# Last sums in two PSUM places, join preparation inside the edge pass, first gathers ahead of the row table

## The reference

```
x = x + gnn(layernorm(x), src, dst)      # 12 heads of 64
x = x + ffn(layernorm(x))

gnn: ft = h W per head;  e = leaky_relu(a1[src] + a2[dst], 0.2)
     w = exp(e - segment_max(e, dst)[dst]);  alpha = w / segment_sum(w, dst)[dst]
     out = relu(segment_sum(alpha * ft[src], dst) + h W_res)
ffn: rows 6..: gelu(x W1 + b1) W2 + b2;  rows 0..5: two gated experts each
```

## Time and profile before

| | us |
|---|---|
| median of 3 runs | 3018.57 |
| lowest, highest | 3011.17, 3021.54 |
| the profiled execution | 3011.33 |
| its span, first to last instruction | 3009.5 |

### The profile page before, as it was taken

The page is one execution under the profiler, slowest core; times in us unless marked ns, Lnnn a source line. Parts: engine busy times, 40 slices in busy tenths (PEclk is TensorE's granted clock), DMA queues, the critical chain, the costliest instruction groups (busy, mean ns, idle before and its releaser), DMA issues. The chain is left out here.

```text
span 3009.5 us, 65141 instructions
## 1 busy us (share of the span) xinstructions
PE 2853.7 (95%) x20124; PEld 2542.5 (84%) x20124; DVE 2488.2 (83%) x5828; ACT 1842.5 (61%) x3384; POOL 2120.1 (70%) x2027
## 2 busy tenths in 40 slices
PE   1999999999999994599999999999999999999998
PEld 1888888888888882488888998898998889898986
DVE  4799999999999966488888888888888888888884
ACT  0666666656566550466666766667666666666762
POOL 6766666666666600578888888888888888888882
PEclk9999999999999997699999999999999999999998
DMA  7999999888887825489888888888888888888873
GB/s 175 171 222 226 211 216 218 217 220 208 215 218 219 218 85 188 148 305 324 312 315 304 306 310 294 304 297 298 302 296 296 294 289 301 291 292 296 290 254 127
DMA packets 246617, 757.83 MB, mean 252 GB/s; under 512 B 78899, under 2 KB 81203, under 8 KB 246291
## 3 DMA queue, kind: packets, MB, share of 16 engines
q1 hardware_dynamic: 176644, 545.08, 51.2%
q0 software_dynamic: 69312, 209.33, 30.3%
q10 hardware_dynamic: 432, 0.62, 0.1%
HBM read 623.04 MB, written 232.17 MB: 284 GB/s over the span
## 5 line engine op out<-in xcount | busy, mean ns | idle before, releaser
L648 ACT ACTIVATE arena<-ps 128x768 f32<-128x768 f32 x392 | 317.9, 811 | 534.7 <-PE ps L708 533.5
L861 PE MATMUL ps<-wr_bd,arena 128*128 128x128 f32 x4704 | 598.4, 277 | 36.0 <-DVE arena L1180 34.6
L861 PEld LDWEIGHTS ps<-wr_bd,arena 128*128 128x128 f32 x4704 | 562.8, 193 | 45.7 <-issue 43.2
L840 PE MATMUL ps<-arena,w_sb 128*96 128x256 f32 x2352 | 571.6, 379 | 0.0
L571 POOL DMA_INDIRECT arena<-agg_scratch,nrow x392 | 439.5, 1121 | 77.7 <-issue 71.9
L1175 DVE SCALAR_TENSOR_TENSOR ps<-ps,r_n,arena 128x768 f32<-128x768 f32 x392 | 400.8, 1022 | 68.5 <-DMA arena<-agg_scratch,nrow 50.5
L840 PEld LDWEIGHTS ps<-arena,w_sb 128*96 128x96 f32 x2352 | 362.3, 163 | 82.8
L551 POOL TENSOR_SCALAR arena<-csr_neg,mv,r_n 128x768 f32<-128x768 f32 x392 | 387.5, 989 | 50.6 <-POOL r_n L579 39.9
L1180 DVE SCALAR_TENSOR_TENSOR arena<-ps,arena 128x768 f32<-128x768 f32 x392 | 375.3, 957 | 13.4
L563 POOL TENSOR_SCALAR arena<-arena,nm_n,r_n 128x768 f32<-128x768 f32 x392 | 383.8, 979 | 1.0 <-issue 0.4
L610 ACT ACTIVATE arena<-ps 128x512 f32<-128x512 f32 x588 | 312.1, 594 | 108.5 <-PE ps L725 70.4
(11 more groups left out here) (197 smaller groups left out, 5502.3 us busy)
## 6 DMA issues: line engine op xcount, KB each, us to landing
arena<-in_x SPq DMA_DIRECT2D x196, 768.0 KB
arena<-in_x_cols SPq DMA_DIRECT2D x392, 384.0 KB
out<-arena SPq DMA_DIRECT2D x195, 768.0 KB, 5.2
agg_scratch<-arena SPq DMA_DIRECT2D x196, 384.0 KB
arena<-in_x,e_slot POOLq DMA_INDIRECT x392
arena<-agg_scratch,nrow POOLq DMA_INDIRECT x392
row_scratch<-e_slot POOLq DMA_INDIRECT x196
nrow<-row_scratch SPq DMA_DIRECT2D x196, 1.0 KB
```

The lines of the kernel that those rows point to most:

```text
L840: last = nc.tensor.matmul(ps[0:HID, 6 + v, 0:PAIR * P], w1_sb[:, i, :], t2[:, v, i, :], start=(i == 0), stop=(i == NC - 1))
L861: last = nc.tensor.matmul(pair(1)[:, i * P:(i + 1) * P], xt_ring[:, g, i * P:(i + 1) * P], wr_bd[:], start=True, stop=True)
```

## The change

- *Sums.* A second PSUM place, `sum2_ps` (banks 3 and 4, those of `ft_ps`), takes every other one of the last ten sums (chunks 186 to 195). From chunk 187 on, a sum waits for the eviction before the last one. The sum of chunk 186 waits for the last eviction of `ft_ps`.
- *Join.* VectorE's preparations stand inside the drain: the comparison of the ends in step 209, the indices in step 211, the scan of maxima in step 213, each behind the message of that step; TensorE's count is in step 210 and has its own place in bank 7. SP loads the ends and the selector in the position of chunk 184. The table's write and its seven loads, and the load of the last rows, are issued by ScalarE instead of SP, so SP goes from the last chunk's write straight to the node loads. The column loop is split in two: all selector matmuls and their copies first (`coef_b` has six blocks), then transposes, scan and transposes back; the waits for first and last rows stand between. GpSimd's wait on `d_fix` stands in front of the first aggregate gather, VectorE's waits on `d_agg` and `d_fix` are gone.
- *Start.* GpSimd doesn't wait for the row table until chunk 7. The scatters of chunks 0 to 6 are issued at chunks 14 to 20, from `e_all`, with a semaphore of their own (`d_scat_first`), beside the scatters of those chunks. VectorE waits, before it fills `e_slot` for group 2, for the gathers of chunk 6.

```diff
-        coef_b = part(19052, 2, 4, EC)
+        coef_b = part(26964, NC, 4, EC)
...
+        def sums(b, co):
+
+            return sum2_ps if isinstance(b, int) and co > EC - L_SUM + L_FT and (EC - 1 - co) % 2 == 1 else sum_ps
+
+        def twice(b, co):
+
+            return 1 if isinstance(b, int) and co > EC - L_SUM + L_FT + 1 else 0
...
+        sum2_ps = ps[:, 3:5, :].rearrange("p a b -> p (a b)")[:, 0:D]
...
+        cnt_ps = ps[0:EH, 7, 2 * P:2 * P + 2]
...
-            sp.dma_start(row_i, dst_ends.rearrange("(o n) e -> o n e", o=1).to_broadcast([P, 2, EC])).then_inc(l_fix, 16)
-            sp.dma_start(sel_sb, sel_heads).then_inc(l_fix, 16)
-            sp.wait_ge(s_tab, NG)
-            sp.dma_start(tab_d, tab[:]).then_inc(d_tab, 16)
-            sp.wait_ge(d_tab, 16)
-            for k in range(G):
-                sp.dma_start(tb.rearrange("h (g k) n -> h g k n", k=G)[:, :, k, :],
-                             tab_d[k * HEADS:(k + 1) * HEADS]).then_inc(l_tab, 16)
-            for u in range(G):
-                sp.wait_ge(d_agg[u], 16 * (EC // G))
-            sp.dma_start(o_last, tail_v[:, :, P - 1, :]).then_inc(d_last, 16)
-            for u in range(2):
-                sp.wait_ge(d_scat[u], 16 * (EC // 2))
+                    if isinstance(b, int) and co_ == EC - 12:
+                        sp.wait_ge(s_ecol, EC)
+                        sp.wait_ge(s_tr, NBLK * EC)
+                        sp.wait_ge(s_ag, 2 * EC)
+                        sp.dma_start(row_i, dst_ends.rearrange("(o n) e -> o n e", o=1).to_broadcast([P, 2, EC]))\
+                            .then_inc(l_fix, 16)
+                        sp.dma_start(sel_sb, sel_heads).then_inc(l_fix, 16)
+
+            sp.wait_ge(d_scat_first, 16 * G)
+            sp.wait_ge(d_scat[0], 16 * (EC // 2 - G))
+            sp.wait_ge(d_scat[1], 16 * (EC // 2))
...
-            pool.wait_ge(d_rowinit, 16)
...
-                        pool.indirect_dma_start(row_d, bass.IndirectOffsetOnAxis(e_slot[:, e, k, 2:3], 0),
-                                                e_slot[:, e, k, 3:4], None, bounds_check=NP - 1, oob_is_err=False)\
-                            .then_inc(d_scat[e], 16)
+                        if isinstance(b, int) and c == G:
+                            pool.wait_ge(d_rowinit, 16)
+                        if isinstance(b, int) and BODY <= c < BODY + G:
+                            pool.indirect_dma_start(row_d, bass.IndirectOffsetOnAxis(e_all[:, i, 2:3], 0),
+                                                    e_all[:, i, 3:4], None, bounds_check=NP - 1, oob_is_err=False)\
+                                .then_inc(d_scat_first, 16)
+                        if not isinstance(b, int) or c >= G:
+                            pool.indirect_dma_start(row_d, bass.IndirectOffsetOnAxis(e_slot[:, e, k, 2:3], 0),
+                                                    e_slot[:, e, k, 3:4], None, bounds_check=NP - 1, oob_is_err=False)\
+                                .then_inc(d_scat[e], 16)
...
-            pool.wait_ge(d_fix, 32)
...
+                        if isinstance(b, int) and tb_ == 0:
+                            pool.wait_ge(d_fix, 32)
...
+            act.wait_ge(s_tab, NG)
+            act.wait_ge(s_tr, NBLK * EC)
+            act.wait_ge(s_ag, 2 * EC)
+            act.dma_start(tab_d, tab[:]).then_inc(d_tab, 16)
+            act.wait_ge(d_tab, 16)
+            for k in range(G):
+                act.dma_start(tb.rearrange("h (g k) n -> h g k n", k=G)[:, :, k, :],
+                              tab_d[k * HEADS:(k + 1) * HEADS]).then_inc(l_tab, 16)
             act.wait_ge(s_gap, 1)
             nc.scalar.activation(gap, gap, ACT.Exp).then_inc(s_gexp, 1)
+            for u in range(G):
+                act.wait_ge(d_agg[u], 16 * (EC // G))
+            act.dma_start(o_last, tail_v[:, :, P - 1, :]).then_inc(d_last, 16)
...
-                at_least(act, s_fixt, j - 1)
-                nc.scalar.activation(coef_b[:, w, :, :].rearrange("p (a b) e -> p a b e", a=2),
+                nc.scalar.activation(coef_b[:, j, :, :].rearrange("p (a b) e -> p a b e", a=2),
...
+            for j in range(NC):
...
-                        at_least(pe, s_eo, co_)
-                        nc.tensor.matmul(sum_ps[:, 0:4 * P].rearrange("p (a f) -> p a f", f=P), mask_ring[:, v, :],
+                        at_least(pe, s_eo, co_ - twice(b, co_))
+                        if isinstance(b, int) and co_ == EC - L_SUM + L_FT + 1:
+                            pe.wait_ge(s_eft, EC)
+                        to = sums(b, co_)
+                        nc.tensor.matmul(to[:, 0:4 * P].rearrange("p (a f) -> p a f", f=P), mask_ring[:, v, :],
                                          ft_ring[:, v, 0:4, 0:P], start=True, stop=True)
...
+                    if isinstance(b, int) and c == EC + 14:
+                        pe.wait_ge(s_eqf, 1)
+                        for n in range(2):
+                            last = nc.tensor.matmul(cnt_ps[:, n:n + 1], eq_f[:, n * EH:(n + 1) * EH], ones[:, 0:1],
+                                                    start=True, stop=True)
+                        last.then_inc(s_cnt, 1)
...
+            pe.wait_ge(s_eo, EC)
+            for j in range(NC):
+                w = j % 2
+                at_least(pe, s_cfe, j - 1)
+                for a in range(4):
+                    last = nc.tensor.matmul(ps[:, 2 * w + a // 2, a % 2 * EC:(a % 2 + 1) * EC], sel_sb[:, j * P:(j + 1) * P],
+                                            coef[:, a, :], start=True, stop=True)
+                last.then_inc(s_ftr, 1)
...
-            pe.wait_ge(s_eo, EC)
...
-                for a in range(4):
-                    nc.tensor.matmul(ps[:, 2 * w + a // 2, a % 2 * EC:(a % 2 + 1) * EC], sel_sb[:, f], coef[:, a, :],
...
-                        at_least(dve, d_scat[q % 2], 16 * G * (b + q // 2))
+                        n_scat = 16 * G * (b + q // 2) - (16 * G if q % 2 == 0 else 0)
+                        at_least(dve, d_scat[q % 2], n_scat)
+                        if isinstance(ge, int) and ge == 2:
+                            dve.wait_ge(d_ge[G - 1], 32)
...
-                                               sum_ps.rearrange("p (c f) -> p c f", f=P), ALU.mult, ALU.add)\
+                                               sums(b, ca).rearrange("p (c f) -> p c f", f=P), ALU.mult, ALU.add)\
...
+                    if isinstance(b, int) and c == EC + 13:
+                        dve.wait_ge(l_fix, 48)
+                        link_up(V.tensor_copy(row_f, row_i))
+                        V.tensor_tensor(eq_f, dstbf[:], row_f[:, 0, :], ALU.is_equal).then_inc(s_eqf, 1)
...
+                        link_up(V.memset(t_run, 1.0))
+                    if isinstance(b, int) and c == EC + 15:
+                        dve.wait_ge(s_cnt, 1)
+                        link_up(V.tensor_tensor(idx_f[:], cnt_ps, cb_sb[:], ALU.add))
+                        V.tensor_copy(idx_i[:], idx_f[:]).then_inc(s_idx, 1)
+                    if isinstance(b, int) and c == EC + 17:
+                        dve.wait_ge(l_tab, 16 * G)
+                        link_up(V.tensor_tensor_scan(m_new, pens[:, 0, :], m_l, -BIG, ALU.add, ALU.max))
...
+                        V.tensor_scalar(gap, gap, 0.0, -100.0, ALU.min, ALU.max).then_inc(s_gap, 1)
...
-            dve.wait_ge(l_fix, 48)
...
-                dve.wait_ge(s_ftr, j + 1)
+                dve.wait_ge(s_ftr, NC + j + 1)
...
-            for u in range(G):
-                dve.wait_ge(d_agg[u], 16 * (EC // G))
-            dve.wait_ge(d_fix, 32)
```

## The result

The changed kernel takes 2990.65 us (median of 4 runs, 2985.14 to 2991.59) against 3018.28 (4 runs, 3011.17 to 3021.54): ratio 0.9908, 95% interval 0.9886 to 0.9929, or 27.6 us less. The forecast was 2987. Its profiled execution took 2989.99 us with a span of 2988.1, 21.3 us less than the one before.

A forecast was written before the change was run, and what follows sets the result against it. TensorE was taken to bound both long passes. Gains of 11.7 us at the start and 19.5 in the join sum to 31.2, from the median of 3018.6 to 2987 us; range 2973 to 3001 for 8 in 10.

The forecast's parts named there:

- What bounds, and that gains arrive whole: Edge and node passes: TensorE bounds both, so time saved at the start or between them arrives at the end whole.
- First gather and first power: Start: first gather at about 7.35 us, 4.4 us earlier; first power at 44.4 us instead of 58.11, 13.7 us earlier.
- The seven scatters come back at chunks 14 to 20 ... I take 2 us: Start: the moved scatters add 1.33 us of GpSimd per chunk; 2 us of the 13.7 gained are given back.
- The sign that the prediction names for it: Start: TensorE gaps at the second and third power longer than before would show the forecast wrong.
- GpSimd doesn't catch up: Start, rival: the scatters cost at chunks 14 to 20 what they saved; only 4.4 us stay, 2995 us; 14%.
- Last sums: Drain: two places cut the step from 2.73 to 1.86 us, bound by VectorE; added work cancels the saving within a microsecond.
- Selector matmuls 17.5 us at 0.50: Join, first half of the split loop: six blocks of 2.91 us, 17.5 us, with the clock staying at 0.50.
- that rival: Join: the clock rises in the selector loop, the matmuls halve after the first block, 7 us more gained, 2980 us; 6%.
- Reload hidden with little to spare: Join: the reloaded rows land by 1190.5 us even behind all node loads, before they are needed at 1192.3.
- rival of a wait that moves in the join: Join: table or reload ends last behind SP's early loads; 3 to 10 us are given back, 2993 us; 12%.
- Split 3.4 us longer by itself, worth it: Join: the split column loop takes 33.0 us instead of 29.6, but the reload lies beside its first half.
- Join 19.5 us: Last eviction to first aggregate gather: 18.2 - 3.4 + 5.0, less roundings, gives 19.5 us; bounds 14 and 26.

The follow-up runs named there:

- second trace: The unmodified changed kernel run and traced once more, on the chip of start alone and join alone: 2988.01 us, ratio 0.9913.
- start alone: The kernel before with only the edits of the start: 3008.97 us, ratio 0.9980.
- filler: The changed kernel with the scatters of chunks 0 to 6 behind GpSimd's edge loop and a small unused power operation at chunks 14 to 20: 2980.02 us.
- one loop: The changed kernel with the column loop put together again, behind the waits for the reloaded rows: 2996.57 us.
- join alone: The changed kernel with the start of the kernel before, so only the last sums and the join are changed: 2995.16 us, ratio 0.9939.
- spread: The changed kernel with VectorE's join preparations dealt out in small portions over steps 209 to 215 instead of blocks: 2984.22 us.
- after: The changed kernel itself, against the kernel before: 2990.65 us, ratio 0.9908.

## Why the prediction was right, and where it was not

- *What bounds, and that gains arrive whole*: right. First aggregate gather 22.0 us earlier, span 21.4.
- *First gather and first power*: right. 8.15 and 44.97 us (7.35 and 44.4 predicted).
- *"The seven scatters come back at chunks 14 to 20 ... I take 2 us"*: this step failed. It was priced by GpSimd's issue time alone. The five chunks took from 55.97 to 87.91, 31.9 us instead of 26.0, and 9.4 us of the 11.8 at chunk 0 were gone at chunk 40 (10.9 of 15.7 in the second trace). What the start earns is 2.4 and 4.8 us in the two traces and 6.0 by the timing of start alone, where 11.7 stood. The filler shows that the issue time, which I priced, costs next to nothing (0.5 us at chunk 40), and that the DMAs, which I priced at nothing, cost about 7 us by the masks. Another 3.6 to 7.3 us of the lead at chunk 0 go without them; the sum had no term for this either. The sign that the prediction names for it was there: TensorE's idle time between chunks 2 and 12 is 6.77 us instead of 3.88. The rival "GpSimd doesn't catch up" had about the right size (4.4 us) but another mechanism: the second power did come late, but GpSimd itself waited there (3.12 and 1.69 us for TensorE's product L792, and 2.29 us of "remote"), and its issue time was not what cost.
- *Last sums*: the mechanism was right, its size was not. Evictions are 1.80 us apart where nothing intervenes (1144.50, 1146.30), so two places do make the step VectorE's. The distance was off by 1.5 and 2.5 us in the two traces. I counted VectorE's work of 3.7 and 3.9 us into the steps and did not ask what TensorE does meanwhile: it idles for 3.33 and 4.03 us, the clock falls, and the next sums take 2.08 us instead of 1.10, too slow for a margin of 0.14 us. With one place they would have been 6 to 7 us longer still; with the work spread they take 21.11 us, less than the 22.4 counted.
- *Table*: right, no wait at the scan.
- *Coefficients 8.8 us after the last eviction*: 8.7 (1165.26 to 1173.98).
- *Selector matmuls 17.5 us at 0.50*: 16.0 us (1173.98 to 1189.95) at 0.50, TensorE 10.00 of 10 us busy in 1175 to 1185. The clock did not rise, so that rival is out. The rule of the Trainium skill that was weighed ("TensorE: Matmul & The Clock Gate", Part 1) would have had it rise here; this trace disagrees, as no slice of this loop shows the clock above 0.50.
- *2.2 us per block*: 2.07 (1190.90, 1192.97).
- *Reload hidden with little to spare*: hidden, with more. It landed 16.1 us after the last eviction in one loop, and the changed kernel asks for it 24.7 us after (1189.95 - 1165.26). I had put it behind all of SP's loads as a worst case. The rival of a wait that moves in the join is out.
- *Split 3.4 us longer by itself, worth it*: against one loop, which has to wait for the reload, it earns 6.0 us.
- *Join 19.5 us*: from the eviction of chunk 187 to the first aggregate gather 71.65 and 70.75 us instead of 90.41, 18.8 and 19.7 us; 18.4 by the timing of join alone. From the last eviction's end to the gather it took 45.8 us where 47.5 were counted, mostly by the loops (30.8 instead of 33.0); that paid for most of the first trace's longer sums. That the sum comes out so close is thus partly luck: two errors cancel.

The forecast of 2987 lay 3.7 us under the measured median. The join was right as a sum; the start was 7 to 9 us too good by the traces. That the whole is nearer than this is luck in part: the forecast gain of 31.2 us stands against 21.3 us between the two profiled executions, 24.4 by the two parts timed alone, 26.2 by the second set of runs and 27.6 by the medians of the first, in which the profiled execution of before lies at the low end, as the prediction says.

## What to carry to other kernels

Price a DMA that is moved into a ramp for what may stall beside it too, not by the issuing engine's 1.3 us alone: seven of them cost about 7 us at mask 40 here. Put it where nobody is close to waiting, here behind the loop. Where an engine's work is gathered into blocks beside a tight chain of matmuls, ask what TensorE does during the block: idle times of 3 to 4 us went with a fall of the clock behind at least one of them in all eight traces, and the matmuls behind them took twice their time. Dealt out in portions, the same work took 1.8 to 3.8 us less. Splitting a loop so that a reload lies beside its first half pays when the reload's landing falls within that half, and a variant with the loop in one piece measures exactly that.

## What the hardware showed beyond this

- The granted clock falls in the ramp beside TensorE's stalls: before at two places (0.78 in 70 to 75 and 0.66 in 75 to 80, with TensorE busy for 1.94 of 5 us in 65 to 70), after at three (0.50 in 60 to 65 and 85 to 90, 0.66 in 105 to 110). In the changed kernel's first trace TensorE's longer busy time makes 4.5 of the 7.4 us lost there.
- The same program does its last sums in 23.95 or 24.89 us; the clock is at 0.50 for 6.8 and for 9.8 us of them.
- In spread TensorE was idle for 8.4 of 21.1 us, in pieces of up to 1.7 us, and the granted clock stayed at 1.00. In after it was idle for 8.5 of 24.9 us, with pieces of 3.3 and 4.0 us, and the clock fell to 0.50 twice.
- Starting the ramp's first transposes 12 us earlier moved chunk 2's mask by 10 to 14 us; another 10.8 us on top (48.59 to 37.77) moved it by 0.4. Chunk 1's mask waits for a signal of TensorE until 62.4 to 63.8 us in the ten traces whose start is early and not paced. Something that no row names limits how early the written-out ramp can be run through.
